# Two transposes of an attention loop, placed two periods later

## The reference, cut to what matters

```python
q = rope((x @ Wq).reshape(b, s, 32, 8)).transpose(0, 2, 1, 3) * scaling
k = rope((x @ Wk).reshape(b, s, 32, 8)).transpose(0, 2, 1, 3)
v = (x @ Wv).reshape(b, s, 16, 16).transpose(0, 2, 1, 3)
probs = softmax(einsum('bhqd,bhkd->bhqk', q, k).astype(float32), axis=-1)
probs = probs.reshape(b, 16, 2, s, s)
w = probs[:, :, 0] - lam * probs[:, :, 1]
attn = einsum('bhqk,bhkd->bhqd', w, v)
```

## Time and profile before

| | before |
|---|---|
| median of 3 runs | 5913.19 us (5902.31 to 5917.62) |
| span of the profiled execution | 5905.1 us |
| attention loop in it | about 467 to 5187 us |
| busy over the whole span: PE, DVE, ACT, POOL | 5596.0, 5463.9, 4958.8, 2055.8 us |
| L813, the 4080 reductions to maxima | 4676.3 us busy |
| L820, the 256 transposes of maxima | 49.4 us busy, 193 ns each |
| L825, the 128 transposes of the sums | 94.1 us busy, 735 ns each |

### The profile page before, as it was taken

How to read it: one execution, slowest core, us unless ns; L and a number is a source line. 1 busy time by engine, 2 the same in 40 slices (tenths; PEclk the granted TensorE clock), 3 DMA queues, 4 the chain that set the end, 5 groups by cost and what they waited for, 6 DMA issues and landing times. The chain is left out here.

```text
span 5905.1 us, 167685 instructions
## 1 busy us (share of the span) xinstructions
PE 5596.0 (95%) x50896; PEld 1970.1 (33%) x50896; DVE 5463.9 (93%) x6142; ACT 4958.8 (84%) x9174; POOL 2055.8 (35%) x3526
## 2 busy tenths in 40 slices
PE   8989999999999999999999999999999999997776
PEld 5542333333333333333333333333333333335425
DVE  7879999999999999999999999999999999977716
ACT  6758999999999999999999999999999999983313
POOL 7972223223332222322333222232333322226506
PEclk9989999999999999999999999999999999998878
DMA  5663222222222222232232222223222222215587
GB/s 194 222 193 58 50 50 52 53 53 53 52 53 52 49 50 51 53 53 53 53 52 53 51 50 51 51 53 53 53 53 53 51 52 51 50 47 183 199 350 301
DMA packets 408166, 495.27 MB, mean 84 GB/s; under 512 B 132051, under 2 KB 265331, under 8 KB 395235
## 3 DMA queue, kind: packets, MB, share of 16 engines
q1 hardware_dynamic: 406499, 485.74, 33.4%
q10 hardware_dynamic: 1024, 0.53, 0.0%
HBM read 360.60 MB, written 123.21 MB: 82 GB/s over the span
## 5 line engine op out<-in xcount | busy, mean ns | idle before, releaser
L813 DVE TENSOR_REDUCE largest<-at_ps_m 128x1 f32<-128x1024 f32 x4080 | 4676.3, 1210 | 45.1 <-PE at_ps_m L925 37.0
L781 ACT ACTIVATE at_e<-at_ps_e 128x512 f32<-128x512 f32 x8192 | 4409.0, 597 | 354.1 <-PE at_ps_e L894 145.0
L911 PE MATMUL at_ps_o<-at_e,at_v 128*32 128x256 f32 (+1 forms) x30720 | 2685.5, 421 | 32.2 <-ACT at_e L781 22.2
L894 PE MATMUL at_ps_e<-w_first 51*128 51x512 bf16 x8192 | 2515.0, 382 | 8.0 <-issue 2.4
L925 PE MATMUL at_ps_m<-w_first 48*128 48x512 bf16 x8160 | 2470.2, 383 | 54.5 <-DVE largest L813 50.5
L911 PEld LDWEIGHTS at_ps_o<-at_e,at_v 128*32 128x32 f32 x30720 | 849.0, 149 | 1566.3 <-issue 824.8
L894 PEld LDWEIGHTS at_ps_e<-w_first 51*128 51x128 bf16 x8192 | 561.2, 93 | 1668.9 <-ACT at_e L781 1637.9
L698 POOL TENSOR_TENSOR at_negated<-at_zeros,at_largest_t 128x32 f32<-128x32 f32 x256 | 64.8, 253 | 2150.6 <-DVE at_largest_t L820 2150.5
L925 PEld LDWEIGHTS at_ps_m<-w_first 48*128 48x128 bf16 x8160 | 564.8, 93 | 171.3 <-DVE largest L813 166.8
L741 POOL TENSOR_TENSOR at_rms<-at_mean_eps,at_minus_half 128x16 f32<-128x16 f32 x128 | 372.7, 2912 | 10.0
L717 POOL TENSOR_TENSOR at_crossed<-at_totals 128x32 f32<-128x32 f32 x128 | 32.4, 253 | 779.4 <-DMA at_totals<-at_sums 779.4
(11 more groups left out here) (131 smaller groups left out, 3042.0 us busy)
## 6 DMA issues: line engine op xcount, KB each, us to landing
w_first<-k_parts SPq DMA_DIRECT2D x1536, 64.0 KB
w_first<-q_parts SPq DMA_DIRECT2D x256, 192.0 KB
w_first<-q_parts SPq DMA_DIRECT2D x256, 128.0 KB
w_first<-in_w SPq DMA_DIRECT2D x32, 1024.0 KB, 23.5
ex_w_second<-in_w SPq DMA_DIRECT2D x32, 1024.0 KB, 25.8
q_parts<-pr_parts SPq DMA_DIRECT2D x96, 256.0 KB, 2.5
k_parts<-pr_parts SPq DMA_DIRECT2D x96, 256.0 KB, 2.5
pr_x_in<-in_x SPq DMA_DIRECT2D x16, 1024.0 KB, 5.7
```

The lines of the kernel that those rows point to most:

```text
L781: nc.scalar.activation(e[:, j % E_BUFS], ps_e[:, bank(u, j)], ACT.Exp, scale=SCALE).then_inc(exp_done, 1)
L813: nc.vector.reduce_max(largest[:, u % 2, j // SIDE, j % SIDE:j % SIDE + 1], ps_m[:, j % 2], AX.X).then_inc(max_done, 1)
L894: nc.tensor.matmul(ps_e[:, bank(u, j)], k_stack[rows, u, pair, c, kt * P:(kt + 1) * P], q_stack[rows, u, pair, c, half * HALF:(half + 1) * ...
L911: last = nc.tensor.matmul(ps_o[32 * tile:32 * tile + 32, columns], v[:, u, tile // 2, first:first + 2 * VD * TILES - kt:TILES], e[:, (QUAD ...
```

## The change

The two calls of `turn_maxima` in DVE's period move from periods 0 and 8 to periods 2 and 10. The first call is for the second half of the quad that is being scored, the other for the first half of the next one.

```diff
                 def period(n, u, g, tries, rows=True, last_quad=True, this_quad=True):
                     if tries:
                         maximum(n + AHEAD, u + AHEAD, 2 * g)
-                    if g == 0 and rows:
+                    if g == LAG and rows:
                         turn_maxima(n, u, 1)
-                    if g == TILES and tries:
+                    if g == TILES + LAG and tries:
                         turn_maxima(n + 1, u + 1, 0)
                     if g == TURN_SUMS and last_quad:
                         turn_sums(n - 1)
```

## The result

The changed kernel takes 6669.72 us (median of 5 runs, 6652.14 to 6675.33) against 5911.06 us before (now the median of 5 runs as well): a ratio of 1.128, 95% interval 1.1268 to 1.1292. It is slower by 759 us; 6606 us were forecast, in a range of 6340 to 6800. The profiled execution spans 6652.0 us, 746.9 us more than before, and does the same 167685 instructions.

What follows compares the result with a forecast made beforehand. DVE was taken to bound the kernel, PE a hair behind. Stall 3.8, gap -0.2 and clock 1.9 make 5.5 us a quad, 693 us in 126 quads; with 5905.1 and 8.1 us, 6606 us, range 6340 to 6800.

Steps and rivals of the forecast that it cites:

- What bounds the kernel: In the attention loop DVE, busy 99.3%, sets the pace with PE a hair behind; time DVE stands still lengthens the run.
- The totals that come too late: At L825 on DVE: six reductions, 6.9 us, cover a chain of 10.64 us, so DVE stalls 3.8 us in 126 quads.
- TensorE's clock: On PE behind the stall: after a 3.7 us pause the clock falls to 0.50 for 4.5 us, costing 1.9 us a quad.
- The gap that is filled: On DVE at each half's long weighted sum: the moved transpose fills a wait, winning 0.11 us, some 0.2 us a quad.
- The sum: Over 126 quads: 3.8 - 0.2 + 1.9 = 5.5 us each, 693 us in all, giving 6606 us.
- The hidden chain: Rival at L825: totals arrive within 6.9 us of the transpose, nothing waits, only the gap is filled: 5888 us; chance 0.05.
- The stall without a fall: Rival on PE: L825 stalls but the clock holds: 6367 us; chance 0.19.
- The second wait: Rival on PE: the first half's rows come late as well, by 2 us in each quad: 6858 us; chance 0.05.

Runs made afterwards that it cites:

- The swap on SP: Changed kernel with the totals of the finished quad moved ahead of the next quad's row load on SP, in the second half: 5894.31 us, ratio 0.9973.
- the run with one period: Kernel before the change with only the second half's transpose of the maxima moved, one period later instead of two: 6024.24 us, ratio 1.0189.

## Why the prediction was right, point by point

**What bounds the kernel.** DVE at 99.3% was the right engine to look at: the 450.8 us of its stall are all in the longer span, and the kernel that fills the gap in period 10 is faster by 9 to 14 us, where 126 x 0.11 = 14 us were reckoned for it.

**The totals that come too late** (3.8 us a quad forecast): right in place, releaser and size. L825's idle time grew by (483.2 - 32.4) / 126 = 3.6 us. The chain of 10.64 us, read from the mean slack in the earlier trace rows, was 10.69 in the quad shown and 10.63 in the mean. The 0.2 us that are missing are on DVE's side: the first of the six reductions starts 0.17 us behind the transpose in the mean, where 0.12 was reckoned, and idle time counts from the end of the last reduction, some 0.1 us behind the point where L825 could start (3044.53 against 3044.44 in the earlier trace rows). The swap on SP takes the stall away with all the transposes where the change put them. L722's wait for L825 fell to 0.86 us each, against 1.72; 0.8 was forecast:

```profile
POOL at_second L722 <- DVE at_crossed_t L825: 109.8, 128, 0.9
```

**TensorE's clock** (1.9 us forecast): right in kind and nearly in size. The fall came in all 126 quads. The Trainium skill, page "TensorE: Matmul & The Clock Gate", section "HAM oscillation — how this bites in real kernels", tells of such a fall in every tile of a kernel whose TensorE waits in every tile. The trace agrees behind these stalls, where PE's pauses are 2.8 to 4.4 us; behind the 0.1 to 1.8 us of the run with one period the fall came 12 times only. The pause was 3.52 us in the quad shown and 3.6 in the mean (3.7 forecast). What was mis-sized is the low stretch: 846 / 127 = 6.7 us, of which 5.8 lie behind the pause and cost time, and not the 4.5 taken. A microsecond of it cost less than the 0.43 reckoned: in the trace the term is the growth of L813's idle time, 243.6 us, less some 20 us that belong to the gap (below), and of its busy time, 35.2 us (waits that are hidden where spans overlap). That makes 2.0 us a quad, 0.35 for each of the 5.8. The two errors nearly cancel.

**The gap that is filled** (-0.2 us): this step failed, in the changed kernel. In the quad shown the reduction behind the second L820 starts 0.30 us behind it (3322.96 to 3323.26), where 0.12 was expected; in the mean of 123 quads it is 0.34, and DVE is idle for 0.13 of these, released by PE's try. With the transposes in period 2 that is some 20 us of idle time in all, 0.2 us a quad lost and not won. The prediction named the condition, that PE bring the try forward with DVE, and it isn't met behind the stall: PE is busy for 5.92 of the 6.00 us there, and the reductions stand 1.14 us apart. That PE is still catching up is the likely reason; no run tests it. Without the stall the step is half right: the gap in period 10 closes and gives some 10 us, while that in period 2, with the totals first, gives nothing that can be measured. The reduction behind the transpose starts 0.18 us behind it there.

**The sum.** 3.6 + 2.0 + 0.2 = 5.8 us a quad against 5.5; 126 quads make 730 us of the 746.9 by which the span grew. The forecast was low by 64 us of 759. The gap makes 45 us of that (25 us to be won, 20 lost), the clock some 20; 17 us stand in none of the terms, and 10 come from the profiled execution, which lies 17.7 us under its median and not 8.1. Against these the stall was 28 us too high. So the sum is nearer than its terms, in part by luck.

**The rivals.** The hidden chain was 3.7 us away from deciding (10.6 us against 6.9), as the prediction had it. The stall without a fall (6367 us) is not what happened, but the run with 17 idle matmuls goes most of the way to it, 6424 us. The second wait does exist, and showed where L825 was moved as well: 27 waits of up to 2.5 us. The prediction argued that in the changed kernel the stall itself keeps it away, since the stores then meet less of the stack loads. The stores do land sooner there, 1.4 us after their issue against 3.0. But the stall isn't needed for it: with the totals first there is none, the stores land after 2.1 us, and one such wait of 0.4 us is left. What else differs where the wait showed is POOL, which begins the split 0.8 us later; which of the two decides was not tried. The row load of the first half, reckoned at 6.90 us behind its transpose from one quad, is issued 5.3 us behind it after the change; the mean before it was 7.8.

## What to carry to other kernels

A step that is moved takes along all that it issues, and what stands behind these issues on in-order queues: here the loss came from a DMA that the diff doesn't name, four totals behind a row load on SP. Before a step is moved, count on each queue the time from it to the next instruction that another engine waits for, and compare it with the work that covers it: 10.7 us of chain under 11.5 us of reductions has 0.8 us to spare, and four reductions are 4.5. Here, where PE is nearly full, a stall of DVE that left it idle for 3.6 us cost twice, 3.6 us as the stall and 2.0 us more as the low clock behind it. The pauses of 0.1 to 1.8 us of the run with one period brought the low clock in 12 quads only.

## What the runs showed of the hardware that was not expected

The granted clock fell after shorter pauses than the one of 3.7 us reckoned with. The loop's end had shown it after 2.40 us. With one period it fell behind 12 pauses of 1.0 to 1.8 us, and did not behind others of up to 1.6 us. With 17 idle matmuls, whose starts stand 0.216 us apart, 31 falls are left, though no single pause at a stall is longer than 1.6 us there. After the falls of the changed kernel the clock stayed at 0.50 for 6.7 us on the average, 0.9 of them while PE was idle anyway.

Idle matmuls that nobody reads made this kernel 245 us faster than it was without them. They are no remedy, since the stall can be taken away, but they measure what the clock costs while the stall stays (472 us against 483).

The landing of small DMAs varies. The same chain of stores, row load and totals took 9.8 to 10.7 us on the average in kernels that differ only in when it starts, and from 9.8 to 11.6 us from quad to quad in the kernel before.
